# Loading the split K and Q of an attention from SBUF to SBUF, without the copy in DRAM

## What is computed

```python
q = layernorm(x) @ Wq + bq            # 100 x 256
k = ctx @ Wk + bk                     # 361 x 256
v = ctx @ Wv + bv
attn = softmax(clip(q_h @ k_h.T * 0.25, -1e4, 1e4))
x = x + concat_h(attn @ v_h) @ Wo + bo
```

## Time and profile before

| | |
|---|---|
| median of three runs | 1069.16 us (1068.76 to 1073.68) |
| the profiled execution | 1067.12 us, of which the span of the trace is 1065.2 us |
| the first attention in it | from the start to about 400 us |
| mean granted TensorE clock | 0.863 |

### The profile page before, as it was taken

One profiled execution on the slowest core, in us unless ns is written; L12 is line 12 of the kernel. 1 busy time (PEld: TensorE's weight loads), 2 busy tenths in 40 slices (PEclk: granted clock), 3 DMA queues, 4 the chain that ended last, 5 costly groups with the idle time before them and its releaser, 6 DMA issues.

```text
span 1065.2 us, 22075 instructions
## 1 busy us (share of the span) xinstructions
PE 837.9 (79%) x7910; PEld 618.8 (58%) x7910; DVE 711.0 (67%) x1453; ACT 550.0 (52%) x1211; POOL 285.9 (27%) x278
## 2 busy tenths in 40 slices
PE   3677778877878758845988999997556889787995
PEld 2355556555656546433765677775214777547995
DVE  7657566666666779631857677654698575776766
ACT  3444555555555434621436555645797465573542
POOL 2345344333434145274000000002643000063300
PEclk9668999999998976775999999998556697998997
DMA  6544455455665449531317556544210000110001
GB/s 164 107 101 98 109 117 123 113 115 116 146 140 118 104 116 338 166 112 52 101 62 227 158 160 192 175 110 140 62 42 9 1 1 0 45 35 2 3 1 62
DMA packets 80152, 107.63 MB, mean 101 GB/s; under 512 B 21217, under 2 KB 62235, under 8 KB 80004
## 3 DMA queue, kind: packets, MB, share of 16 engines
q1 hardware_dynamic: 71824, 93.66, 33.1%
q0 software_dynamic: 5248, 10.67, 3.2%
q10 hardware_dynamic: 3012, 2.41, 0.8%
HBM read 85.58 MB, written 20.92 MB: 100 GB/s over the span
## 4 chain that ended last, share of the span: by engine, by line
PE 45%; DVE 17%; issue 14%; DMA 9%; ACT 8%; POOL 3%; ACTq 3%; SPq 1%; DVEq 0%; POOLq 0%; another core or an unknown queue 0%
PE ps L1148 11%; PE ps L1135 9%; PE ps L1655 3%; PE ps L427 3%; DMA floor<-floor_q 2%; PE ps L522 2%; PE ps L2099 2%; POOL mTl L475 2%; PE ps L1649 2%; ACTq L484 2%; DVE pmax L1616 1%; DMA xe<-floor 1%; PE ps L2110 1%; PE ps L556 1%; PE ps L598 1%
## 5 line engine op out<-in xcount | busy, mean ns | idle before, releaser
L509 DVE TENSOR_REDUCE m<-ps 100x2 f32<-100x722 f32 x128 | 115.7, 907 | 92.0 <-PE ps L504 90.6
L1197 ACT ACTIVATE hT<-ps,cols 128x500 f32<-128x500 f32 (+1 forms) x96 | 62.5, 651 | 128.8 <-PE ps L1135 95.1
L544 DVE SCALAR_TENSOR_TENSOR p<-p,xe 121x600 f32<-121x600 f32 x128 | 104.3, 816 | 14.0 <-DMA xe<-floor 13.9
L529 ACT ACTIVATE p<-ps 121x600 f32<-121x600 f32 x128 | 85.5, 668 | 54.4 <-PE ps L522 53.4
L1204 DVE TENSOR_TENSOR hT_l<-hT,hT_h 128x500 f16<-128x500 f32 (+1 forms) x96 | 62.4, 652 | 75.9 <-ACT hT_h L1198 59.2
L1148 PE MATMUL ps<-w_h,hT_h 128*125 128x256 f16 (+1 forms) x384 | 105.5, 275 | 1.8 <-DVE x L1244 1.2
L1148 PE MATMUL ps<-w_l,hT_h 128*125 128x256 f16 (+1 forms) x384 | 105.4, 275 | 0.0
L1148 PE MATMUL ps<-w_h,hT_l 128*125 128x256 f16 (+1 forms) x384 | 105.4, 274 | 0.0
L1492 POOL PARTITION_ALL_REDUCE gmax<-cmax x6 | 2.2, 367 | 357.9 <-DVE cmax L1487 351.8
L1135 PE MATMUL ps<-xe_h,w_h 128*128 128x500 f16 (+1 forms) x192 | 73.0, 380 | 23.2 <-issue 10.0
L522 PE MATMUL ps<-qs,ks 128*121 128x100 f16 x768 | 71.6, 234 | 21.5 <-ACT p L529 11.2
(11 more groups left out here) (332 smaller groups left out, 2160.6 us busy)
## 6 DMA issues: line engine op xcount, KB each, us to landing
xe<-floor SPq DMA_DIRECT2D x32, 378.1 KB
sw<-in_L_ffn_w_dram SPq DMA_DIRECT2D x16, 512.0 KB, 7.6
sw<-in_L_ffn_w_dram SPq DMA_DIRECT2D x8, 1024.0 KB, 5.8
stage<-in_L_xattn_W_f_dram SPq DMA_DIRECT2D x6, 1024.0 KB, 8.2
k_parts<-kp SPq DMA_DIRECT2D x32, 181.5 KB, 3.5
ks<-k_parts SPq DMA_DIRECT2D x32, 181.5 KB
ctx_f<-in_ctxT_dram SPq DMA_DIRECT2D x16, 270.8 KB, 4.6
stage<-in_ctxT_dram SPq DMA_DIRECT2D x8, 541.5 KB, 8.9
```

Of the source, the lines that this page charges most:

```text
L509: v.tensor_reduce(m32[p][:, 2 * i:2 * i + 2], ps[0:T, at:at + 2, 0:KV], AX.X, ALU.max).then_inc(m_max, 1)
L529: s.activation(p32[:, i % HALF, :, :, :].rearrange("p j n t -> p n j t"), ps[0:KT, t_bank(i):t_bank(i) + 2, 0:KJ * T].rearrange("p n (j t) ...
L544: v.scalar_tensor_tensor(probs, probs, 1.0, low, ALU.min, ALU.max).then_inc(a_cv, 1)
L1197: s.activation(hT[:, f % 3, 0:m], bank[2 + f % 2][:, 0:m], ACT.Silu, bias=bias, scale=1.0 / WS)
```

## The change

`k_store`, `q_store` and the DRAM tensors `k_parts` and `q_parts` go. `half_load` now reads `kp` and `qp` in SBUF directly, with seven DMAs a half: three of K, each from 128 partitions of 363 elements to 16 partitions of 8 x 363; three of Q, each from 128 partitions of 100 elements to 16 partitions of 8 x 100; and one that puts the two zero rows into `qs`. It waits for `k_l` and `q_l`, the marks of the low parts, instead of for the stores. As the loads now read `kp` and `qp`, these may be overwritten only when the loads have landed: `k_high` (ACT) waits for the loads of the batch before, and `qp` gets a second buffer, with `q_gpsimd` waiting for the loads of two batches before. The counts of `sel_in` and of the loads (`heads_in` in place of `loaded`) follow.

```diff
-        def k_store(sp, b, t, p, c):
-            sp.wait_ge(k_l, 2 * b + c + 1)
-            wait(sp, (kq_in, k1_in)[c][p], 64 * t)
-            wait(sp, k_out, 16 * (2 * b + c))
-            sp.dma_start(k_d[p, c].rearrange("n p k -> p n k"), kp[:, :, c, :]).then_inc(k_out, 16)
...
-        def k_high(s, b, c):
+        def heads_in(t):
+            return 16 * 7 * (t + 1)
+
+        def k_high(s, b, t, p, c):
             s.wait_ge(k_32, 2 * b + c + 1)
-            wait(s, k_out, 16 * (2 * b + c - 1))
+            wait(s, (kq_in, k1_in)[c][1 - p], heads_in(t + p - 1))
             s.copy(kp[:, 0, c, 0:KV], k32[c][:, :]).then_inc(k_h, 1)
...
-        def q_gpsimd(g, b):
+        def q_gpsimd(g, b, t, p):
             g.wait_ge(q_32, b + 1)
-            wait(g, q_out, 32 * b)
+            for half in (kq_in, k1_in):
+                wait(g, half[p], heads_in(t - 1))
...
-        def q_store(sp, b, t, p):
-            sp.wait_ge(q_l, b + 1)
-            for half in (kq_in, k1_in):
-                wait(sp, half[p], 64 * t)
-            wait(sp, q_out, 32 * b)
-            for c in range(CC):
-                sp.dma_start(q_d[p, c, 0:2 * 128].rearrange("(n p) t -> p n t", n=2), qp[:, :, c, :]).then_inc(q_out, 16)
...
         def half_load(sp, b, p, c):
             done = (kq_in, k1_in)[c][p]
             heads = slice(c * NP, (c + 1) * NP)
-            sp.wait_ge(k_out, 16 * (2 * b + c + 1))
-            k_hl = k_d[p, c].rearrange("n (d h) k -> (n d) (h k)", h=NP)
-            sp.dma_start(ks[p][0:2 * D, heads, :].rearrange("p h k -> p (h k)"), k_hl).then_inc(done, 16)
-            sp.dma_start(ks[p][2 * D:3 * D, heads, :].rearrange("p h k -> p (h k)"), k_hl[0:D]).then_inc(done, 16)
-            sp.wait_ge(q_out, 32 * (b + 1))
-            q_hl0 = q_d[p, c].rearrange("(r h) t -> r (h t)", h=NP)
-            sp.dma_start(qs[p][0:D, heads, :].rearrange("p h t -> p (h t)"), q_hl0[0:D]).then_inc(done, 16)
-            sp.dma_start(qs[p][D:ROW_M + 2, heads, :].rearrange("p h t -> p (h t)"), q_hl0).then_inc(done, 16)
+            sp.wait_ge(k_l, 2 * b + c + 1)
+            for at, n in ((0, 0), (1, 1), (2, 0)):
+                sp.dma_start(ks[p][at * D:(at + 1) * D, heads, :], kp[:, n, c, :]).then_inc(done, 16)
+            sp.wait_ge(q_l, b + 1)
+            for at, n in ((0, 0), (1, 0), (2, 1)):
+                sp.dma_start(qs[p][at * D:(at + 1) * D, heads, :], qp[p][:, n, c, :]).then_inc(done, 16)
+            sp.dma_start(qs[p][ROW_M:ROW_M + 2, heads, :], qs[0][ROW_M + 16:ROW_M + 18, 0:NP, :]).then_inc(done, 16)
...
             sp.wait_ge(k_pad, 1)
-            for c in range(CC):
-                k_store(sp, 0, 0, 0, c)
             context_load(sp, 2, 0)
-            q_store(sp, 0, 0, 0)
-            sp.wait_ge(sel_in, 64)
             for c in range(CC):
                 half_load(sp, 0, 0, c)
             sp.dma_start(ks_flat[1][48:128, :], a["pick_h"]).then_inc(k_pad, 16)
             context_load(sp, 3, 1)
-            for c in range(CC):
-                k_store(sp, 1, 0, 1, c)
-            q_store(sp, 1, 0, 1)
             sp.wait_ge(k_pad, 17)
             half_load(sp, 1, 1, 0)
             floor_load(sp, 0, 0)
```

More of the change, by code:

```diff
@@ L225, in build @@
         q32 = sba("q32", [128, CC, T])
-        qp = sba("qp", [128, 2, CC, T], F16)
+        qp = [sba(f"qp{p}", [128, 2, CC, T], F16) for p in range(2)]
         ks_flat = [sba(f"ks{p}", [128, H * KP], F16) for p in range(2)]
@@ L231, in build @@
         qs = [sba(f"qs{p}", [128, H, T], F16) for p in range(2)]
-        k_d = nc.dram_tensor("k_parts", (2, CC, 2, 128, KP), F16, kind="Internal").ap()
-        q_d = nc.dram_tensor("q_parts", (2, CC, 2 * 128 + H, T), F16, kind="Internal").ap()
         floor_d = nc.dram_tensor("floor", (2, T * H // 2), F32, kind="Internal").ap()
@@ L281, in build @@
         o_r, o_32, o_n = (sem(f"o_{n}") for n in ("r", "32", "n"))
-        k_out, q_out = sem("k_out"), sem("q_out")
         den_dma = sem("den_dma")
@@ L385, in q_scalar @@
             i.then_inc(q_32, 1)
-        def q_gpsimd(g, b):
+        def q_gpsimd(g, b, t, p):
             g.wait_ge(q_32, b + 1)
-            wait(g, q_out, 32 * b)
-            g.tensor_tensor(qp[:, 0, :, :].rearrange("p c t -> p (c t)"), q32[:, :, :].rearrange("p c t -> p (c t)"),
+            for half in (kq_in, k1_in):
+                wait(g, half[p], heads_in(t - 1))
+            g.tensor_tensor(qp[p][:, 0, :, :].rearrange("p c t -> p (c t)"), q32[:, :, :].rearrange("p c t -> p (c t)"),
                             ones_col.broadcast_to((128, CC * T)), ALU.mult).then_inc(q_h, 1)
             g.wait_ge(q_h, b + 1)
-            g.tensor_tensor(qp[:, 1, :, :], q32[:, :, :], qp[:, 0, :, :], ALU.subtract).then_inc(q_l, 1)
-        def q_store(sp, b, t, p):
-            sp.wait_ge(q_l, b + 1)
-            for half in (kq_in, k1_in):
-                wait(sp, half[p], 64 * t)
-            wait(sp, q_out, 32 * b)
-            for c in range(CC):
-                sp.dma_start(q_d[p, c, 0:2 * 128].rearrange("(n p) t -> p n t", n=2), qp[:, :, c, :]).then_inc(q_out, 16)
+            g.tensor_tensor(qp[p][:, 1, :, :], q32[:, :, :], qp[p][:, 0, :, :], ALU.subtract).then_inc(q_l, 1)
         def half_load(sp, b, p, c):
@@ L499, in s_tensor @@
             if i % HALF == 0:
-                pe.wait_ge((kq_in, k1_in)[i // HALF][p], loaded(t))
+                pe.wait_ge((kq_in, k1_in)[i // HALF][p], heads_in(t))
             wait(pe, m_max, before)
@@ L699, in a_scalar @@
                 if i in (2, 6) and has(b, 2):
-                    k_high(s, b + 2, i // HALF)
+                    k_high(s, b + 2, t + 1, p, i // HALF)
                 if i in (4, 5) and has(b, 3):
@@ L733, in a_gpsimd @@
                     if has(b, 2):
-                        q_gpsimd(g, b + 2)
+                        q_gpsimd(g, b + 2, t + 1, p)
                 if i == 1 and not has(b, 1):
@@ L762, in a_sync @@
                 half_load(sp, b + 1, q, 1)
-            if has(b, 2):
-                q_store(sp, b + 2, t + 1, p)
             floor_load(sp, b, 1)
@@ L771, in a_sync @@
             if has(b, 2):
-                k_store(sp, b + 2, t + 1, p, 0)
                 sp.wait_ge(a_s, NP * b + HALF)
@@ L780, in a_sync @@
                 inv_store(sp, b - 1)
-            if has(b, 2):
-                k_store(sp, b + 2, t + 1, p, 1)
             if not has(b, 2):
@@ L891, in even_load @@
             sp.wait_ge(c_l, 2 * B)
-            sp.wait_ge(sel_in, 80)
+            sp.wait_ge(sel_in, 16)
             for n in ns:
@@ L899, in guard_even_gpsimd @@
             g.wait_ge(x_in[n], 48)
-            wait(g, sel_in, 80 + n)
+            wait(g, sel_in, 16 + n)
             part = xn[:, LB * n:LB * (n + 1), :]
@@ L905, in guard_select @@
             v.wait_ge(y_x, LB * (n + 1))
-            v.wait_ge(sel_in, 80 + n + 1)
+            v.wait_ge(sel_in, 16 + n + 1)
             v.wait_ge(yb_ev, 7)
@@ L2318, in _ @@
                 c_gpsimd(g, 1, 1, c)
-            q_gpsimd(g, 0)
+            q_gpsimd(g, 0, 0, 0)
             g.memset(zeros[:, :, :], 0.0)
@@ L2324, in _ @@
                 k_gpsimd(g, 1, c)
-            q_gpsimd(g, 1)
+            q_gpsimd(g, 1, 0, 1)
             for c in range(2):
@@ L2372, in _ @@
                 k_scalar(s, 0, 0, c)
-                k_high(s, 0, c)
+                k_high(s, 0, 0, 0, c)
             s.wait_ge(a_pad, 1)
@@ L2387, in _ @@
                 k_scalar(s, 1, 1, c)
-                k_high(s, 1, c)
+                k_high(s, 1, 0, 1, c)
             open_std(s, 2)
@@ L2488, in _ @@
             sp.wait_ge(a_pad, 1)
-            for p in range(2):
-                for c in range(CC):
-                    sp.dma_start(q_d[p, c, 2 * 128:2 * 128 + H], qs[0][ROW_M + 16:ROW_M + 18, 0:NP, :]).then_inc(sel_in, 16)
             sp.wait_ge(k_pad, 1)
-            for c in range(CC):
-                k_store(sp, 0, 0, 0, c)
             context_load(sp, 2, 0)
-            q_store(sp, 0, 0, 0)
-            sp.wait_ge(sel_in, 64)
             for c in range(CC):
```

## The result

The changed kernel takes **1081.54 us** (median of 20 runs), the kernel before beside it 1068.84: ratio **1.0112**, 95% interval 1.0086 to 1.0138. It is slower, by 12.7 us, where 1062 was forecast, and the range up to 1073 did not hold it. The profiled execution took 1085.14 us, its span is 1083.3.

The account below looks back on a forecast made before the run. Bound by a ring of waits between PE, ACT and DMAs. Steady loop -5.1, opening -1.2, end -1.0 sum to -7.3 us: profiled 1067.12 becomes 1059.8, as a median 1062 us; range 1052 to 1073.

Parts of the forecast that it names:

- A ring of waits: First attention's batch loop: no engine is full; waits of PE and ACT that K or Q DMAs cause count.
- What is removed: Per batch, four stores and two 34-partition loads go; DMA work falls from 60 engine-us plus Q loads to 40 to 45.
- The copy was hidden anyway: Whole kernel: the change does what it says and gives 0, 1069 us; lower end of the narrower gain, no own chance.
- The tail on two engines goes: Steady loop: without the 34-partition Q load, waits of 3.7 us for `mTl` and 1.4 for Q go; -5.1 us.
- The size of an issue: SP's queue: 0.45 us a DMA, between 0.28 and 0.64, so a half's seven take 3.2 us.
- The pieces: Added per batch: 768 K pieces of 726 B at 36 ns, 768 Q pieces of 200 B at 16 ns; 40 engine-us.
- The new waits in the loop: `k_high` on ACT and `q_gpsimd` on GpSimd wait for loads that PE has already used: zero cost.
- The opening: Start of the kernel: later `k_high` on ACT against an earlier floor load; -1.2 us, bounds +2.1 and -1.8.
- The 1.0 us at the end: Near 362 us, a floor store behind the last K and Q load lands sooner: -1.0 us, between 0 and -2.4.
- The narrow writes: K DMAs writing to 16 partitions hold queue time up, so only -3 us, 1066 us; chance 0.27.
- The larger gain: Fewer waits remove some drops of PE's clock; five drops and DVE's 3.8 us add 10 us: 1052 us; chance 0.13.
- The slower case: Seven loads a half make half 1 late if a DMA needs over 0.74 us; 1087 us, milder 1075; chance 0.12.

Follow-up runs that it names:

- the new order: Half 1's load issued ahead of the inverse's load: changed kernel 0.9894, again 0.9940; kernel before with the same order 0.9922 and 0.9930.
- the three loads from DRAM: Kernel before with each half of K loaded from DRAM by three DMAs to 16 partitions each, instead of two to 32 and 16: 0.9984.

## Why the prediction was wrong, point by point

- **What bounds the kernel.** A ring of waits between PE, ACT and the DMAs was right as far as it went. Missed was that the ring's price is paid in clock. The text named it at the end, "a hundredth of PE's 838 busy us is 8 us, as much as the sum", and gave it no case of its own on the slow side.
- **What is removed.** Right: the stores and SP's wait for K's store are gone, and the DMA share in the loop is 0.44 where "near 0.45" was forecast. It was worth nothing: the new order with and without the direct move gives 0.9940 and 0.9930. That is the rival "The copy was hidden anyway", which got no chance of its own.
- **The step that failed: "The tail on two engines goes, so `mTl` lands near 236 to 238, before 239.5".** The share of 0.13 in the earlier trace rows was read as the one tail there is. Behind it stood another, on four engines: the inverse's load, issued right ahead of half 1 in both kernels. `mTl` took 6.8 us instead of 6.7 from issue to PE (233.76 to 240.46), not the 2 to 4 forecast. With `rden` split it takes 3.2, and 3.9 at most. And the rows of the half that isn't behind `rden`, which the prediction left as they were, went from 1.7 us to 3.4 to 4.7. Instead of gaining 5.1 us in its steady part, the loop lost 12.7 over 14 iterations.
- **The size of an issue.** Taken 0.45 us, measured 0.63; it was the upper bound, 0.64. A half's seven take 4.5 us, not 3.2. The last of them, issued at 219.18, released PE at 225.03, 5.9 us later, where the sum took the shortest landing, 2.1.
- **The pieces.** The fall of the DMA share came out as forecast, but by luck: two sizes were wrong and cancel. In 130 to 330 us of the kernel after a piece of 726 B takes 66 ns and one of 200 B 25 ns by the trace's packet records, not 36 and 16, so a batch needs some 70 engine-us and not 40. The K loads that they replace took 497 ns a row of 5,808 B, 48 engine-us a batch and not 33, and a piece of the Q stores 25 ns as well. The place of the pieces was not looked at: three DMAs of 128 small pieces give each of the four laden engines as much to do behind `rden` as any other engine. Why that hurts more than the larger rows of before is not shown. What the traces show is that `rden` itself lands 7.0 to 7.5 us after its issue, before 5.8 to 6.2, and that with `rden` split the pieces don't hurt.
- **The new waits in the loop.** Right: `k_high` doesn't wait for a load in 130 to 330 us, so the zero holds.
- **The opening.** `k_high` of batch 1, half 1, waits 0.90 us and runs at 38.66 us, 3.2 later than in the earlier trace rows: the stated cost at 0.64 us an issue, +3.0. The first floor load is issued at 55.96 instead of 53.07. No gain of 1.2, but 1.1 us lost by the first reciprocal, and the run with two pairs of `kp` shows that it doesn't matter: the loop gave its 3.5 us back. The 1.0 us at the end wasn't measured by itself.
- **The rivals.** The narrow writes (0.27) are refuted as a cause by the three loads from DRAM, if it makes no difference that these read DRAM. The larger gain (0.13) had the right lever and the wrong sign for this order: the clock's share in 132 to 332 us went from 0.94 to 0.88, and the new order, with 0.97 to 0.99, is what it describes. The slower case (0.12) had the place right, half 1 and what it holds back, and its point wrong: it was to need 0.74 us a DMA, while 0.63 was enough, since landing took 5.9 us and not 2.1. Its price, lateness times 14, left out the clock. The bound was drawn from the shortest landing in the trace, and here an unbalanced DMA stood ahead of it.

## What to carry to other kernels

Before a DMA is moved or added, look at what is issued just ahead of it, and on how many engines each goes; here a broadcast load from four rows kept four engines busy long after the others, and the small transfers behind it waited for them, so try to split such a load by rows or to issue it later. In a loop where PE has gaps, price a new gap by the granted clock of the windows behind it, not by its length. And test the order of a queue before a path: here the order gave 0.6 to 1.1% with either path, and the path itself nothing.

## What was not expected of the hardware

- An SBUF to SBUF DMA of 128 pieces took 0.63 us to issue on SP, for pieces of 726 and of 200 bytes alike, and the one of the zero rows, 16 pieces, 0.65; loads from DRAM with longer rows took 0.28 to 0.43.
- Contracting over 48 rows instead of 128, with zeros in the rest, slowed the whole kernel by 2.9%, through a granted clock of 0.85 instead of 0.92 in the loop; PE was busy 262.3 us instead of 229.5 with as many matmuls.
- One load of 200 KB in 128 pieces of 1,600 bytes from four rows landed 7.0 to 7.5 us after its issue in the kernel after; as four DMAs of 32 pieces each, 3.4 us after the first issue in the iteration shown, though another 1.3 us of issuing is in it.
